# A write of 320 words behind each gather on GpSimd, and table blocks stored by one transfer

## The reference

```python
def rgcn_conv(x, edge_index, edge_type, W, root, bias):
    src, dst = edge_index
    out = x @ root + bias
    for r in range(8):
        mask = edge_type == r
        h = x @ W[r]
        msg = jnp.where(mask[:, None], h[src], 0)
        agg = segment_sum(msg, dst, N)
        cnt = segment_sum(mask, dst, N)
        out = out + agg / jnp.maximum(cnt, 1.0)[:, None]
    return out

h = relu(layernorm(x))
for W, root, b in three_layers:
    h = relu(rgcn_conv(h, edge_index, edge_type, W, root, b))
x = x + h
h = relu(layernorm(x))
a = h + segment_sum(h[src], dst, N)
a = relu(a @ W1 + b1) @ W2 + b2
x = x + batchnorm(a) * gamma + beta + h
```

## Time and profile before

| | |
|---|---|
| median of 3 runs | 1913.76 us (1910.78 to 1917.29) |
| profiled execution | 1917.36 us |
| its span, first to last instruction | 1915.3 us |
| mean granted TensorE clock | 0.633 of full speed |
| POOL busy | 1201.2 us (63%) |
| PE / PEld busy | 1209.7 / 856.7 us |
| DVE / ACT busy | 843.3 / 636.2 us |
| last gather begins | 1872.33 us |

### The profile page before, as it was taken

One profiled execution on the slowest core, in us unless ns is written; L12 is line 12 of the kernel. 1 busy time (PEld: TensorE's weight loads), 2 busy tenths in 40 slices (PEclk: granted clock), 3 DMA queues, 4 the chain that ended last, 5 costly groups with the idle time before them and its releaser, 6 DMA issues.

```text
span 1915.3 us, 17586 instructions
## 1 busy us (share of the span) xinstructions
PE 1209.7 (63%) x4604; PEld 856.7 (45%) x4627; DVE 843.3 (44%) x3270; ACT 636.2 (33%) x1147; POOL 1201.2 (63%) x1350
## 2 busy tenths in 40 slices
PE   6798764655565565656565656567566565656667
PEld 2266443434344354444444444446344444444444
DVE  4566575355444245655556566552121212122123
ACT  5310500000000256766767676752011020202133
POOL 5755666666666656666666666656666666666660
PEclk9697855555555655656565556565567676756688
DMA  7552333233322311222222222231111111111111
GB/s 226 180 159 89 85 113 93 78 106 89 93 87 73 101 38 43 84 51 79 57 72 61 72 64 67 66 93 47 44 47 44 50 43 48 46 45 44 47 47 40
DMA packets 80802, 144.19 MB, mean 75 GB/s; under 512 B 24687, under 2 KB 38248, under 8 KB 80696
## 3 DMA queue, kind: packets, MB, share of 16 engines
q0 software_dynamic: 39840, 81.67, 17.3%
q1 hardware_dynamic: 40424, 60.68, 9.2%
q10 hardware_dynamic: 432, 0.64, 0.1%
HBM read 100.23 MB, written 42.67 MB: 75 GB/s over the span
## 4 chain that ended last, share of the span: by engine, by line
another core or an unknown queue 29%; PE 25%; issue 15%; POOL 14%; DVE 7%; ACT 6%; DMA 2%; DVEq 0%; SPq 0%; ACTq 0%; POOLq 0%
POOL rows L1250 14%; PE ps_agg L561 7%; PE ps_h L530 6%; PE ps_a L648 4%; DVE early L1059 3%; ACT scratch L845 3%; DMA rows<-h_table,idx 2%; DVE sel L963 2%; PE ps_agg L616 1%; PE ps_a L579 1%; DVE scratch L1048 1%; PE ps_a L668 1%; PE ps_h L668 1%; ACT early L1337 1%
## 5 line engine op out<-in xcount | busy, mean ns | idle before, releaser
L1250 POOL DMA_INDIRECT rows<-h_table,idx x1175 | 1118.7, 952 | 631.2 <-issue 323.8
L561 PE MATMUL ps_agg<-sel,rows 128*128 128x64 f32 (+14 forms) x2764 | 664.8, 362 | 280.2 <-DMA rows<-h_table,idx 210.3
L561 PEld LDWEIGHTS ps_agg<-sel,rows 128*128 128x128 f32 x2764 | 625.2, 287 | 459.3 <-DMA rows<-h_table,idx 245.6
L963 DVE TENSOR_SCALAR sel<-iota,early,norm 128x64 f32<-128x64 f32 x1178 | 357.0, 334 | 427.1 <-PE ps_agg L561 208.8
L648 PE MATMUL ps_a<-scratch 128*128 128x300 bf16 x416 | 165.5, 399 | 255.7 <-DVE early L1059 142.5
L1059 DVE TENSOR_TENSOR early<-ps_a,early 128x300 f32 x416 | 195.9, 471 | 261.7 <-remote 177.2
L845 ACT ACTIVATE scratch<-scratch,ones 128x300 bf16<-128x300 f32 x416 | 221.2, 532 | 161.7 <-remote 129.2
L530 PE MATMUL ps_h<-w_all,xT 128*128 128x512 f32 x300 | 220.7, 849 | 59.7 <-issue 24.1
L851 ACT ACTIVATE scratch<-iota,code_lo 128x300 f32<-128x300 f32 x416 | 226.5, 545 | 12.5
L941 DVE TENSOR_SCALAR_CACHE_REDUCE agg_s<-scratch,key_f 128x256 bf16<-128x256 int16 x416 | 193.5, 472 | 31.5 <-issue 20.5
L648 PEld LDWEIGHTS ps_a<-scratch 128*128 128x128 bf16 x416 | 59.7, 144 | 296.9 <-issue 283.6
(11 more groups left out here) (158 smaller groups left out, 739.7 us busy)
## 6 DMA issues: line engine op xcount, KB each, us to landing
h_table<-stage SPq DMA_DIRECT2D x130, 256.0 KB
rows<-h_table,idx POOLq DMA_INDIRECT x1175
scratch<-key_rows SPq DMA_DIRECT2D x26, 544.0 KB
h_table<-scratch SPq DMA_DIRECT2D x20, 256.0 KB
x_rows<-in_x SPq DMA_DIRECT2D x6, 256.0 KB, 6.1
w_all<-in_W SPq DMA_DIRECT2D x3, 512.0 KB, 6.7
x_table<-early SPq DMA_DIRECT2D x6, 256.0 KB, 2.3
out<-early SPq DMA_DIRECT2D x6, 256.0 KB
```

The source lines that it names most:

```text
L561: mm = nc.tensor.matmul(sums_of(L, k)[:, at:at + width], mine, sel[edges, G % SELS, in_window:in_window + width], start=False, stop=(t == ...
L963: done = nc.vector.tensor_scalar(mine, here, dst, weight, ALU.is_equal, ALU.mult)
L1250: pool.indirect_dma_start(rows[:, slot, :], None, table, bass.IndirectOffsetOnAxis(ap=column, axis=0)).then_inc(landed, 16)
```

## The change

GpSimd gets a private area `slow` of two times 320 words a partition. Behind each gather of the layers (and in place of the three gathers that SyncE does) it writes 320 zeros in every partition. Nobody reads them. The two halves of the area are used in turn, and an even tile's memset waits until the odd one before it has finished, by the semaphore `s_rested`. The other edit: a block of a table is stored by one transfer of 512 KB when both halves are there; `s_stage` therefore counts 16 a store and not 32, in all places that wait for it.

```diff
+PAUSE = 320
...
+        slow = sb("slow", [P, 2, PAUSE])
...
             if stores_of(slot_of[H], H):
-                eng.wait_ge(s_stage[slot_of[H]], 32 * stores_of(slot_of[H], H))
+                eng.wait_ge(s_stage[slot_of[H]], 16 * stores_of(slot_of[H], H))
...
             sp.wait_ge(s_evA, H + 1)
-            sp.dma_start(rows_out[:, 0:4, :], rows_in[:, 0:4, :]).then_inc(s_stage[slot_of[H]], 16)
             sp.wait_ge(s_evD, H + 1)
-            sp.dma_start(rows_out[:, 4:8, :], rows_in[:, 4:8, :]).then_inc(s_stage[slot_of[H]], 16)
+            sp.dma_start(rows_out, rows_in).then_inc(s_stage[slot_of[H]], 16)
...
+            def rest_a_while(G):
+
+                if G % 2 == 0 and G > FORE:
+                    pool.wait_ge(s_rested, (G - FORE) // 2)
+                done = nc.gpsimd.memset(slow[:, G % 2, :], 0.0)
+                if G % 2 == 1:
+                    done.then_inc(s_rested, 1)
+
...
                         if G in END_TILES:
+                            rest_a_while(G)
                             continue
...
                             gather(L, G % SLOTS, idx[:, t:t + 1], s_row[G % SLOTS])
+                        rest_a_while(G)
```

More of the change, by code:

```diff
@@ L412, in gnn_kernel @@
         s_beat = sem("s_beat")
+        s_rested = sem("s_rested")
         s_row = [sem(f"s_row{n}") for n in range(SLOTS)]
@@ L813, in fill @@
                 for n in range(STAGES):
-                    act.wait_ge(s_stage[n], 32 * stores_of(n, BLOCKS * GIN))
+                    act.wait_ge(s_stage[n], 16 * stores_of(n, BLOCKS * GIN))
             if b >= FILLS:
@@ L927, in late_tile @@
                 for n in range(STAGES, ALL_STAGES):
-                    dve.wait_ge(s_stage[n], 32 * stores_of(n, BLOCKS))
+                    dve.wait_ge(s_stage[n], 16 * stores_of(n, BLOCKS))
             if t >= 2:
@@ L1113, in wait_table @@
             for n in range(ALL_STAGES):
-                pool.wait_ge(s_stage[n], 32 * stores_of(n, BLOCKS * (L + 1)))
+                pool.wait_ge(s_stage[n], 16 * stores_of(n, BLOCKS * (L + 1)))
         SP_BRANCH = 7
@@ L1258, in _ @@
                         for n in range(ALL_STAGES):
-                            pool.wait_ge(s_stage[n], 32 * stores_of(n, table_of(L, late_blocks[0])))
+                            pool.wait_ge(s_stage[n], 16 * stores_of(n, table_of(L, late_blocks[0])))
                         pool.wait_ge(s_late_made, 1)
```

## The result

The changed kernel takes 1949.1 us (median of 4 runs, 1944.4 to 1953.7); the kernel before took 1915.5 in the same measurement. The ratio is 1.017, 95% interval 1.014 to 1.020: slower by 1.7%, where 2% faster was forecast. In the profiled executions the span grew from 1915.3 to 1948.0 us, by 32.7.

The account below looks back on a forecast made before the run. GpSimd's gathers were taken to set the pace, slowed by a shared path and stops. Pitch 1.42 us gave -43 us, the store +3, total -40: 1874 us; forecast's own range 1850 to 1893, overall range 1828 to 1937.

Parts of the forecast that it names:

- GpSimd's own pitch: Time from one gather to the next with the memset between, as GpSimd alone allows: 1.25 to 1.64 us.
- the gather at 78.26: Earlier trace: it started before the stretched memset pair ended at 78.35, read as gathers not waiting for a memset's end.
- the fourth of the five bounds: GpSimd's pitch as 0.95 + 0.39 + 0.15 = 1.49 us, the idle time behind the memset coming on top.
- rival 1: Pause too long, GpSimd's own pitch binds without stalls; at 1.49 us, +41 + 3, 1958 us; chance 0.26.
- 1.41 us for a gather more and 0.46 us for the stop itself: GpSimd's layers: a gather costs 1.41 us on something shared; each stop adds 0.46 us, which the pause would save.
- 1196 x 1.42 = 1698 us: All gathers of the three layers at the forecast pitch of 1.42 us, with the stops' extra 0.46 us gone.
- The memset's 0.39 us: Estimated time of one 320-word memset on GpSimd: 0.12 + 0.27 us, bounded by 0.48 us above.
- remote: GpSimd's gathers' idle time of that kind, 187 us, would mostly go or become small waits on the memset.
- the 14 us of the late sums: Two GpSimd waits while TensorE sums late blocks' edges would remain, some 14 us beyond a normal pitch.
- The store's +3 us: One 512 KB store per block delays gathers waiting for a table; +3 us taken, bounds -2 to +4.
- The wait for `s_rested`: Even gathers' memsets wait for the one before, a brake holding GpSimd back a little when signals are late.
- The rule of the Trainium skill on the shared port: GpSimd and a two-port VectorE tensor_scalar exclude each other; a memset meeting one would wait some 0.2 us.

Follow-up runs that it names:

- e3: The changed kernel with memsets of 200 words instead of 320: 1922.6 us, ratio 1.0027 to the kernel before.
- e14: The changed kernel with memsets of 240 words instead of 320: ratio 1.0006 (0.9981 to 1.0030) to the kernel before.
- e4: The changed kernel with memsets of 96 words instead of 320: 1920.7 us, ratio 1.0019 to the kernel before.
- e2: The changed kernel without its memsets, only the single store per block: 1915.6 us, ratio 1.0003 (0.9976 to 1.0029) to the kernel before.

## Why the prediction was wrong

**What failed first: the pitch.** I bounded GpSimd's own pitch from 1.25 to 1.64 us and let the gather at 78.26, which started before its memset's end, decide for 1.25 to 1.34. The measured pitch is 0.95 + 0.38 + 0.17 = 1.50, the fourth of the five bounds and the 1.49 of rival 1. The idle time behind the memset is 0.16 to 0.17 us with 200, 256 and 320 words alike, and also behind a memset that VectorE stretches (710.73, 0.47 us, then 0.16). The pair of one-word memsets at 77.65 was stretched too, but what was late there didn't hold the next gather. Shown singly, its second memset and the one of the undisturbed pair at 87.78 are these:

```profile
78.01 0.34 POOL L1236 MEMSET beat<- 128x1 f32 x1
87.96 0.10 POOL L1236 MEMSET beat<- 128x1 f32 x1
```

The next gathers start at 78.26 and 88.21, both 0.25 us after the start of that memset: only the memset's end was late at 78.26, and the row held no sign that a gather overlaps a memset of any length. That one row showed a tiny memset and was no row for one of 320 words; the regular ones of the earlier trace rows, with 0.15 us behind the second beat every time, were the nearer, and I had them.

**What failed second: the price.** Had the pitch been 1.42, the forecast would still have missed: 1.40 (e3) and 1.43 to 1.44 (e14) gained nothing. "1.41 us for a gather more and 0.46 us for the stop itself" was drawn through two runs from two different layers, 10 gathers in layer 1 and 22 in layer 0. The stop has no price of its own: e3 and e4 made the stops rarer (53 and 92 instead of 114), and the mean stayed. Each run with its stop costs 14.54 / 10 = 1.454 in layer 1 and 31.43 / 22 = 1.429 in layer 0, and that is the price. The 0.46 us of each stop were not there to be had. The term "1196 x 1.42 = 1698 us" should have been no less than the 1755 measured before, and the forecast's own case was empty: a pitch below the price gives the time of before, one above it a loss.

**What held.** The memset's 0.39 us (386 ns). The stops vanish where the pitch is long enough, and with them "remote": in layer 1 ScalarE's 129 us (L845) and VectorE's 177 us (L1059) of it before are gone too. Rival 1 was the mechanism: 1.49 us, +41 for the layers (measured +43.9), and "GpSimd then never stalls, but its own pitch is the bound"; it got 0.26. Two errors cancel in the +41: the pitch came to 1.504 us by the windows (1799.2 / 1196), stretched memsets among them, and the 14 us of the late sums that I let remain went too (all that TensorE holds a gather is 8.6 us). Its 1958 us are 9 above the result mostly because the ends gave 11 back: they follow TensorE's distance, which I had left out of every case. The store's +3 us are not seen in e2, whose interval of some 5 us either way holds all of its bounds of -2 to +4, so that term stays unmeasured. The wait for `s_rested`, which I counted as a brake, bound nothing (0.6 us in all). The rule of the Trainium skill on the shared port (SBUF — State Buffer, "Who interferes with whom") showed seldom: in 150 to 650, 700 to 1200 and 1300 to 1850 us 27 of 1030 memsets took over 0.42 us, each begun while a tensor_scalar of VectorE ran, though most that began so were not stretched. They take up to 0.56 us (in layers 1 and 2 up to 0.47) where most take 0.38, and are too few to matter: the mean is 386 ns.

## What to carry to other kernels

Where an engine runs fast, stops, and runs fast again, take run and stop together as its price before you credit a smoother pace with anything: here, spreading the same work evenly cost and gained nothing below that price, and lost above it. To see which it is, change the pitch in two or three sizes and look at the mean, not at the stops. And when a new instruction goes between two others, take its place in the gap from the regular rows, not from one odd one.

## What the runs showed of the hardware

- A gather by index of 128 rows from GpSimd has a price near 1.43 us in layers 0 and 2 (1.45 to 1.50 as the mean of a whole layer), far over the 0.95 us that the profile shows as busy; it is the same with 64 rows or 256 bytes a row (1.41 to 1.44). While gathers follow each other faster, the other engines' signals come late at times (4.5 us in the earlier trace rows). A plain DMA of 128 rows takes GpSimd 0.54 us, and tiles then pass in 0.72 us.
- GpSimd's memset: 200 ns for 96 words, 284 for 200, 331 for 256, 386 for 320, so 0.83 ns a word and 0.12 us besides; 0.16 to 0.17 us pass between its end and the next gather, for all four sizes.
- Running further ahead is not free here: 24 tiles instead of 12 cost 1.8%, some 36 us, and the stretches between the layers and behind the last gather are 36 us longer than in the trace of before (86.7 against 50.4). The number of stops hardly changes with the distance (104, 114 and 112 with 24, 12 and 6 tiles).
